# The D term and the gate of a selective-scan layer: moved from the matmul array to VectorE and GpSimd

## The reference

```python
y = jnp.swapaxes(ys, 0, 1) + D[None, None, :, None] * xh
y = y.reshape(batch, L, D_INNER) * jax.nn.silu(z)
return residual + jnp.einsum('bli,di->bld', y, out_proj_w)
```

## Time and profile before

| | |
|---|---|
| time, median of 3 runs | 274.05 us (271.35 to 275.15) |
| span of the profiled execution | 268.5 us |
| PE busy | 217.8 us, 81% |
| DVE busy | 166.4 us, 62% |
| ACT busy | 125.4 us, 47% |
| POOL busy | 49.3 us, 18% |
| chain that ended last | PE 54%, DVE 34%, ACT 4%, issue 4% |

### The profile page before, as it was taken

The page is one execution under the profiler, slowest core; times in us unless marked ns, Lnnn a source line. Parts: engine busy times, 40 slices in busy tenths (PEclk is TensorE's granted clock), DMA queues, the critical chain, the costliest instruction groups (busy, mean ns, idle before and its releaser), DMA issues.

```text
span 268.5 us, 3677 instructions
## 1 busy us (share of the span) xinstructions
PE 217.8 (81%) x1077; PEld 133.8 (50%) x1077; DVE 166.4 (62%) x480; ACT 125.4 (47%) x266; POOL 49.3 (18%) x92
## 2 busy tenths in 40 slices
PE   3412989599686985898599967988899999998894
PEld 0212536465443763655456634756444544443794
DVE  2786799898879999599989788495011020202243
ACT  2524455563144565457445036655854536180451
POOL 5136900001443269100001161000000000000000
PEclk9855699999978899999999979999999999999999
DMA  6350000020041000000050000000005050310022
GB/s 187 80 193 1 0 0 0 10 75 4 1 142 53 0 1 2 0 0 1 4 158 2 1 0 0 2 0 0 0 7 150 2 156 0 116 40 0 14 67 78
DMA packets 13487, 10.40 MB, mean 39 GB/s; under 512 B 1582, under 2 KB 11287, under 8 KB 13471
## 3 DMA queue, kind: packets, MB, share of 16 engines
q1 hardware_dynamic: 10982, 9.02, 11.2%
q10 hardware_dynamic: 2488, 1.19, 1.9%
HBM read 9.08 MB, written 1.07 MB: 38 GB/s over the span
## 4 chain that ended last, share of the span: by engine, by line
PE 54%; DVE 34%; issue 4%; ACT 4%; DMA 1%; POOL 1%; DVEq 0%; ACTq 0%; POOLq 0%
PE bank L558 48%; DVE xcT L1252 6%; DVE cmax L1363 2%; DVE rmax L1353 2%; DVE xhT L1288 2%; DVE zsT L1285 2%; DVE bst L1098 2%; DVE hh L1183 2%; DVE hh L1175 2%; DVE dv L1236 2%; DVE xntok L1206 1%; DVE BT L1379 1%; DMA eo<-in_L_wmod_dram 1%; DVE diag_c L1366 1%; PE bank L852 1%
## 5 line engine op out<-in xcount | busy, mean ns | idle before, releaser
L1400 DVE SCALAR_TENSOR_TENSOR seg_e<-bank,vecT,gbT 128x512 f32<-128x512 f32 x8 | 6.0, 751 | 54.4 <-PE bank L558 54.4
L558 PE MATMUL bank<-slotsT,w_sb 128*128 (+1 forms) x64 | 28.4, 596 | 0.8 <-issue 0.8
L558 PE MATMUL bank<-eo,xhT 128*128 (+1 forms) x192 | 23.1, 277 | 5.4 <-DVE xhT L1335 4.3
L558 PE MATMUL bank<-xnT,winT 128*128 128x512 f32 x48 | 25.1, 649 | 2.2 <-ACT BT L954 1.9
L558 PEld LDWEIGHTS bank<-eo,xhT 128*128 128x128 f32 x192 | 22.1, 191 | 6.8 <-DVE xhT L1335 4.8
L1037 ACT ACTIVATE zsT<-bank,vecT 128x512 f32<-128x512 f32 x16 | 11.0, 688 | 21.2 <-PE bank L558 20.9
L508 POOL TENSOR_TENSOR root<-root,neg_half 128x2 f32<-128x2 f32 (+1 forms) x24 | 20.5, 855 | 2.0
L503 POOL TENSOR_SCALAR root<-mv 128x2 f32<-128x2 f32 (+1 forms) x12 | 3.3, 277 | 94.4 <-DVE mv L1102 89.2
L558 PEld LDWEIGHTS bank<-slotsT,w_sb 128*128 128x128 f32 x64 | 11.6, 190 | 16.5 <-issue 15.5
L987 ACT ACTIVATE seg_e<-bank 128x512 f32<-128x512 f32 x24 | 12.8, 598 | 13.7 <-PE bank L558 13.6
L558 PE MATMUL bank<-snT,CTr 128*128 128x512 f32 x32 | 18.5, 707 | 0.9 <-ACT CTr L944 0.9
(11 more groups left out here) (166 smaller groups left out, 412.3 us busy)
## 6 DMA issues: line engine op xcount, KB each, us to landing
w_sb<-in_L_ffn_w_dram SPq DMA_DIRECT2D x16, 256.0 KB, 3.0
mods_bc<-mod_dram SPq DMA_DIRECT2D x8, 320.0 KB, 3.7
xin<-in_L_attn_x_dram SPq DMA_DIRECT2D x4, 256.0 KB, 3.9
out_dram<-xin SPq DMA_DIRECT2D x8, 128.0 KB, 1.8
eo<-in_L_wmod_dram ACTq DMA_DIRECT2D x1, 384.0 KB, 3.4
eo<-in_L_attn_in_proj_w_dram ACTq DMA_DIRECT2D x1, 384.0 KB
eo<-n_L_ffn_slot_embeds_dram ACTq DMA_DIRECT2D x1, 256.0 KB, 4.6
eo<-n_L_attn_out_proj_w_dram ACTq DMA_DIRECT2D x1, 128.0 KB
```

Source lines behind the costliest of these rows:

```text
L558: return nc.tensor.matmul(o, lhsT, rhs, start=start, stop=stop)
L1400: V.scalar_tensor_tensor(eoT[:, :, j, :], bank[4 + j][:, :].rearrange("p (b s) -> p b s", b=B), vecT[:, bass.ds(it * 2 + (RB2 + j), 1)], g ...
```

## The change

The D matmuls and diag_d go. `y_of` now waits for all weighings of its batch before its first matmul, and gives out the matmuls of both heads of a group in turns. VectorE's `gate` becomes two instructions per batch, one for each group of channels: `xhT = xhT * D/2 + bank`. A new visit of GpSimd, `gate_z`, multiplies xhT by silu(z) in place, and `project_out` waits for that. On GpSimd the due times of the four root visits are new, and their own semaphores become one.

```diff
-        diag_d = spare[:, 0, :, :]
...
+        yd_done = sem("yd_done", 2)
...
-        pool_own_var = sem("pool_own_var", 2)
-        pool_own_ms = sem("pool_own_ms", 2)
+        pool_own2 = sem("pool_own2", 4)
...
+            def gate_z(bi):
+                def visit(j, it):
+
+                    wait(pool, yd_done, j, it, bi + 1)
+                    hold(pool)
+                    v = (slice(None), slice(None), slice(bi * L, (bi + 1) * L))
+                    nc.gpsimd.tensor_tensor(xhT[j][v], xhT[j][v], zsT[j][v], ALU.mult).then_inc(yg_done[1][j], 1)
+                return visit
+
...
-            visits = [(-23.59, var_root1), (-14.84, ms_root1), (-0.21, add_basis), (3.06, gate_weights),
-                      (15.9, var_root(0)), (55.17, var_root(1)), (56.18, ms_root(0)), (56.2, ms_root(1))]
+            visits = [(-23.59, var_root1), (-14.84, ms_root1), (-0.21, add_basis), (3.06, gate_weights), (36.4, gate_z(0)), (42.8, gate_z(1)),
+                      (39.5, var_root(0)), (44.5, var_root(1)), (48.0, ms_root(0)), (51.0, ms_root(1))]
...
                     wait(pe, dtx_done, j, it, bi + 1)
+                    wait(pe, m_done, j, it, 3 * bi + 3)
                     for k in range(CT):
-
-                        mm(bank[4 * j + bi][:, k * L:(k + 1) * L], diag_d[:, k, :], xhT[j][:, k, bi * L:(bi + 1) * L],
-                           stop=False)
-                        if k == 0:
-                            wait(pe, m_done, j, it, 3 * bi + 3)
                         for h in (2 * k, 2 * k + 1):
                             o = bank[4 * j + bi][(h % 2) * HD:(h % 2 + 1) * HD, k * L:(k + 1) * L]
-                            mm(o, dtx[j][:, bi * NT, h * HD:(h + 1) * HD],
-                               seg_m[j][:, k, (h % 2) * L:(h % 2 + 1) * L], start=False, stop=False)
-                            q = mm(o[:, P:L], dtx[j][:, bi * NT + 1, h * HD:(h + 1) * HD],
-                                   seg_m[j][:, 2, tile_cols(h)], start=False)
+                            nc.tensor.matmul(o, dtx[j][:, bi * NT, h * HD:(h + 1) * HD],
+                                             seg_m[j][:, k, (h % 2) * L:(h % 2 + 1) * L],
+                                             start=k == 0, stop=False, skip_group_check=True)
+                        for h in (2 * k, 2 * k + 1):
+                            o = bank[4 * j + bi][(h % 2) * HD:(h % 2 + 1) * HD, k * L:(k + 1) * L]
+                            q = nc.tensor.matmul(o[:, P:L], dtx[j][:, bi * NT + 1, h * HD:(h + 1) * HD],
+                                                 seg_m[j][:, 2, tile_cols(h)],
+                                                 start=False, stop=k == CT - 1, skip_group_check=True)
                     q.then_inc(y_ps[1][j], 1)
...
-            for k in range(CT):
-                V.tensor_scalar(diag_d[:, k, :], ident[:, :], d_half[:, k:k + 1], None, ALU.mult)
...
                     wait(dve, y_ps, j, it, bi + 1)
-                    v = (slice(None), slice(None), slice(bi * L, (bi + 1) * L))
-                    V.tensor_tensor(xhT[j][v], bank[4 * j + bi][:, :].rearrange("p (k t) -> p k t", k=CT), zsT[j][v],
-                                    ALU.mult).then_inc(yg_done[1][j], 1)
+                    for k in range(CT):
+                        t = slice(bi * L, (bi + 1) * L)
+                        q = V.scalar_tensor_tensor(xhT[j][:, k, t], xhT[j][:, k, t], d_half[:, k:k + 1],
+                                                   bank[4 * j + bi][:, k * L:(k + 1) * L], ALU.mult, ALU.add)
+                    q.then_inc(yd_done[1][j], 1)
```

More of the change, by code:

```diff
@@ L496, in _, with inverse_root @@
             pool.wait_ge(s_ready, 3)
-            def inverse_root(kind, done, own, ready, src, k, tiles):
+            def inverse_root(kind, done, own, ready, src, k, tiles, own_at=1):
                 def visit(j, it):
@@ L505, in visit @@
                                             ALU.max if kind == 2 else ALU.add).then_inc(own[1][j], 1)
-                    at = 2 if ready is root_done and kind == 1 else k
+                    at = 2 if ready is root_done and kind == 1 else own_at
                     wait(pool, own, j, it, at)
@@ L512, in var_root @@
             def var_root(bi):
-                return inverse_root(0, var2_done, pool_own_var, var_root_done, variances, bi + 1, of_batch(bi))
+                return inverse_root(0, var2_done, pool_own2, var_root_done, variances, bi + 1, of_batch(bi), bi + 1)
             def ms_root(bi):
-                return inverse_root(2, ms2_done, pool_own_ms, ms_root_done, mean_squares, bi + 1, of_batch(bi))
+                return inverse_root(2, ms2_done, pool_own2, ms_root_done, mean_squares, bi + 1, of_batch(bi), bi + 3)
             def add_basis(j, it):
```

## The result

The changed kernel takes 283.53 us (median of 4 runs, 283.37 to 285.23), the kernel before 274.60 (4 runs, 271.35 to 275.16): ratio 1.038, 95% interval 1.031 to 1.046. The ratios in this text are formed from the undisturbed executions alone, so they are not the quotients of the medians beside them (here 1.033). A second set of runs of the same file gave 1.039 (1.025 to 1.054). The forecast was 282.5, slower, range 276 to 287.

The account below looks back on a forecast made before the run. It took VectorE, nearly always busy and coupled to TensorE, to limit the kernel. Two turns of 4.5 us less 0.4 for setup made 8.6 on the median 274.05: 282.6 us, given as 282.5, range 276 to 287.

Parts of the forecast that it names:

- The bound: Stretch of y and projections: TensorE and VectorE are coupled; freeing TensorE buys at most VectorE's idle time, 1.48 us.
- the view of the chain of waits: Stretch of y and projections: TensorE alone sets it, so its 9.8 us saved would give 264; faster outcomes 0.05.
- The y visit: TensorE's y matmuls: a visit goes from 2.85 to 1.62 us without the diagonal products; reordering the heads' matmuls counts 0.
- VectorE's pair: VectorE's gate as two instructions of 256 columns: holds VectorE about 0.68 us, done after 0.76, where one took 0.69.
- The product: GpSimd's multiplication of 512 columns between gate and projection: about 1.30 us each time, from the basis addition's mean.
- Hand-overs: Around GpSimd's product: VectorE to GpSimd 0.20 us, GpSimd to TensorE 0.06 us.
- The setup: Before the turns: VectorE drops two products, saving 0.4 us of at most 0.48.
- The walk: One turn followed gate by gate: delays grow from 1.4 us at the first x1 to 4.5 at the row maximum.
- The hold: VectorE's two-input instructions beside GpSimd's product: each that meets one is held its full 1.30 us.
- latency only: Rival: GpSimd's product costs by its length, VectorE is never held; 2.2 us a turn, 278 us; chance 0.20.
- The wait for the root behind the last product: GpSimd's root for pair 0's unit2 stands behind the product: 1.0 us more, unit2 at 78.4, was 73.94.
- third rival: TensorE's clock also falls after idle pieces of about 3 us before projections: 1.2 us a turn, 285 us; chance 0.12.

Follow-up runs that it names:

- experiment 1: Kernel before without the products with the diagonal, D term left out, nothing in their place: 270.62 us against 271.88, ratio 0.997.
- experiment 2: Changed kernel, GpSimd's product replaced by a power of few columns, product with gate left out: six columns 279.63 to 290.0 us; five 280.69 us, ratio 1.031.

## Why the prediction was right, and where it was not

**The bound.** Right. TensorE's time for the D products, 9.8 us in the forecast, was worth 0.3% (experiment 1), the view of the chain of waits, with two pieces of 12.14 us of matmuls, notwithstanding.

**The terms.** The y visit came to 1.45 us, forecast 1.62. That is not the new order of the matmuls: in the old order, without the D products, the same eight take 1.47 (experiment 1), so the order gives 0.02 and what was wrong is the subtraction; without the D products the first visit of before loses 1.38, not 1.23. It mattered little, since TensorE's time was not what was waited for. VectorE's pair holds it for 0.78 (57.86 to 58.64) and is done after 0.86, forecast 0.68 and 0.76. The product takes 1.26 alone, forecast 1.30, and 1.54 where a VectorE instruction is still running. Hand-overs are 0.18 and 0.06, forecast 0.20 and 0.06. The setup gave 0.1, forecast 0.4. The 0.4 is there (from d_half to the next instruction behind it 0.19 us, before 0.59), but in this execution VectorE's work ahead of it had started 0.30 later (14.58, before 14.28).

**The walk.** Forecast and measured: x1 0/0 62.5, 62.12; gate 0/1 64.6, 64.25; gate of pair 0 batch 1 68.9, 68.38; x1 of pair 0 batch 1 72.5, 72.11; last gate 75.1, 74.88; unit2 78.4, 78.26; second unit2 82.6, 82.48; row maximum 84.2, 84.40; logits 79.9, 79.96. The first gate came 0.22 early, which is most of the constant difference, so behind the first gate the row maximum came 0.4 later than forecast; the places of the two late roots are met within 0.15.

**The hold.** Right in size where it falls (1.07 and 1.0 of 1.26) and right as the sign of the change; wrong as the main cause. I had priced "latency only" at 2.2 us a turn and so the hold at 2.3; measured, the length alone is 3.7 and 4.1, and the hold adds 1.35 and 1.58 to it. The step that failed is in that rival's walk: it put gate 1 of pair 0 at 66.45, 8.37 behind the first gate, as if the first x1 could stay where it was. But x1 0/0 itself waits for the first projection, which waits for the first product (0.48 <-PE in experiment 2), so it came 0.74 later than before and that gate at 9.01. Of the rest, about 0.4 is the third projection at the low clock (1.62 us in place of 1.16) and 0.35 lies behind unit2. The wait for the root behind the last product was priced about rightly (unit2 3.4 behind the last gate, measured 3.45). The Trainium skill, "SBUF — State Buffer", section "Who interferes with whom", has VectorE instructions with two SBUF inputs and GpSimd take turns at the ports. The weighings of 3.56 against 2.49 us agree. The power of few columns agrees one way only: it holds no weighing (2.49 in both power versions), as the prediction had seen for its smaller like, but it is held by them, once for four weighings (3.42 us in experiment 2).

**The clock.** A part of the third rival came true beside the forecast: TensorE waits 1.5 to 2.7 us before each projection, and behind such pieces the low clock shows more often (slices of 5 to 7 tenths in the page of after). It cost 0.7 us on x26 and 1.8 on x48 in the profiled execution, and 0.7 on the third projection of the second turn (x1 waits 1.60 us for it, 0.86 in the first). On the logits it cost only 0.2 (3.78 us, before 3.55), since they were at the low clock before as well. The forecast had put this term at nothing; it measured 3.2 to 3.4 of the 13.4 us between the spans. That the idle pieces are its cause is argued, not shown: executions of the unchanged kernel differ in their clock too.

**The sum.** 8.6 us forecast, against 8.9 between the medians, 10.5 by the ratio, and 13.4 between the two profiled spans. Two errors cancelled in it. I took 5.5 us around the span, since I held the profiled execution for a typical one; 1.7 is right, and the execution was one of the shortest, so my starting point of 274.05 us was 3.9 above what it took (about 270.2). And a turn costs 5.0 to 5.7, not 4.5, with the clock besides, so the sum was 4.8 short of the 13.4. That the number came within 1.0 us is in part luck; sign, place and order of each step are not.

## What to carry to other kernels

A matmul that rides in a chain of matmuls may cost nothing: before moving it, leave it out and time that, to see what its time on TensorE is worth there (0.3% here). Work put between two engines that hand over closely delays both and what stands behind it on its new engine (3.7 and 4.1 us a turn here for its length alone), and GpSimd was a dearer place for it than VectorE (1.038 against 1.021), since VectorE had two-input work queued. Place such a product only where the slack to its consumer is longer than it is; here one place of four had that, and there the change cost nothing.

## What the runs showed of the hardware

- The contention has two outcomes from one place: a product that asked 0.26 to 0.27 us into a weighing got the next turn (1.54 us, a weighing held 1.07), or waited out four weighings (3.35 us, none held).
- A GpSimd product of 512 columns took 1.26 us and VectorE's own 0.69.
- A GpSimd power of 5 columns took 1.16 to 1.46 us, about as long as a product of 512, and held no weighing. It can be held itself: one of 6 columns, 1.32 us elsewhere, took 3.42 beside four weighings.
- The low clock moves between executions: four passes of logits took 1.98 us in one turn and 2.3 to 3.8 in the others, and executions of the unchanged kernel spread from 270.3 to 277.1 us.
